# Sums over masked keys in an attention stage: two float32r passes over the high and low parts of the values, split by GpSimd batch by batch

## What is computed

```python
def _L0_xattn_ref(value, key, query, mask, Wv, bv, Wk, bk, Wq, bq, Wo, bo):
    v = (value @ Wv.T + bv).reshape(n, -1, H, D)
    k = (key @ Wk.T + bk).reshape(n, -1, H, D)
    q = (query @ Wq.T + bq).reshape(n, -1, H, D)
    qk = jnp.einsum('nqhd,nkhd->nhqk', q, k)
    qk = jnp.where(mask == 0, jnp.asarray(1e-20, qk.dtype), qk)
    attn = jax.nn.softmax(qk / jnp.asarray(np.sqrt(E), qk.dtype), axis=3)
    out = jnp.einsum('nhqk,nkhd->nqhd', attn, v).reshape(n, q_len, H * D)
    return out @ Wo.T + bo
...
x = x + _L0_xattn_ref(ctx_1024, ctx_1024, _layernorm(x, axis=-1), mask_Bx1xSxS2_ik1, ...)
```

## Time and profile before

| | |
|---|---|
| median of 3 runs | 4522.49 us (4519.5 to 4533.23) |
| span of the profiled execution, the only time of its own that the page gives | 4527.3 us |
| TensorE busy | 3886.3 us (86%) |
| VectorE busy | 3074.1 us (68%) |
| ScalarE busy | 2057.9 us (45%) |
| GpSimd busy | 795.1 us (18%) |
| granted TensorE clock, mean over the span | 0.907 |
| loop of the first attention | from 126.8 to about 772 us of the span |

### The profile page before, as it was taken

How to read it: one execution, slowest core, us unless ns; L and a number is a source line. 1 busy time by engine, 2 the same in 40 slices (tenths; PEclk the granted TensorE clock), 3 DMA queues, 4 the chain that set the end, 5 groups by cost and what they waited for, 6 DMA issues and landing times. The chain is left out here.

```text
span 4527.3 us, 83053 instructions
## 1 busy us (share of the span) xinstructions
PE 3886.3 (86%) x30431; PEld 2824.0 (62%) x30525; DVE 3074.1 (68%) x7110; ACT 2057.9 (45%) x3636; POOL 795.1 (18%) x510
## 2 busy tenths in 40 slices
PE   6799997799377999796399999779997987999899
PEld 5344443798365777575378888635555665555577
DVE  7666664456746666544566666678867887888587
ACT  3355554233103333342044444347775762777510
POOL 6433321401431000000023322410000013000000
PEclk9799999599668999897599999879998998999999
DMA  8233331201311000011054544722210015222000
GB/s 266 86 100 101 101 91 54 68 26 42 125 62 33 19 19 19 28 40 37 13 158 124 132 125 125 230 80 66 66 38 19 1 35 199 60 67 67 28 19 19
DMA packets 234478, 338.02 MB, mean 75 GB/s; under 512 B 39204, under 2 KB 132950, under 8 KB 234167
## 3 DMA queue, kind: packets, MB, share of 16 engines
q1 hardware_dynamic: 218280, 306.66, 21.4%
q0 software_dynamic: 15888, 27.23, 2.8%
HBM read 242.42 MB, written 107.01 MB: 77 GB/s over the span
## 5 line engine op out<-in xcount | busy, mean ns | idle before, releaser
L1918 ACT ACTIVATE a_pT<-a_psS 128x512 f32<-128x512 f32 x1536 | 836.0, 597 | 387.7 <-PE a_psS L1804 382.4
L1990 DVE TENSOR_REDUCE a_mx<-a_psA 128x1 f32<-128x512 f32 x1024 | 656.4, 685 | 82.9 <-PE a_psA L1782 82.8
L1819 PE MATMUL a_psZ<-a_pT,a_V 128*17 128x128 f32 x12288 | 488.8, 278 | 0.0
L1782 PE MATMUL a_psA<-a_ks,a_qs 48*128 48x512 f32 (+1 forms) x1536 | 405.5, 523 | 83.8 <-DVE a_mx L1990 36.9
L1986 DVE CUSTOM_DVE_ANT_0 a_scored<-a_psA,a_hide_q 128x512 bf16<-128x512 f32 x512 | 332.7, 688 | 184.4 <-PE a_psA L1782 183.3
L1819 PEld LDWEIGHTS a_psZ<-a_pT,a_V 128*17 128x17 f32 x12288 | 272.8, 97 | 272.7 <-issue 163.3
L1782 PEld LDWEIGHTS a_psA<-a_ks,a_qs 48*128 48x128 f32 (+1 forms) x1536 | 151.6, 192 | 330.2 <-DVE a_mx L1990 127.7
L1804 PE MATMUL a_psS<-a_qs,a_ks 50*128 50x512 f32 (+1 forms) x1536 | 318.3, 408 | 2.7 <-ACT a_pT L1918 0.8
L3262 DVE SCALAR_TENSOR_TENSOR ex_h<-ex_psU,ex_ub,ex_sg 128x512 f32<-128x512 f32 x129 | 96.9, 751 | 189.3 <-PE ex_psU L159 182.3
L2002 POOL TENSOR_TENSOR X<-X,a_osb 128x512 f32<-128x512 f32 x48 | 61.1, 1278 | 935.3 <-ACT a_osb L1905 917.3
L3208 ACT CAST ex_w_h<-X 128x1024 fp32r<-128x1024 f32 x102 | 106.0, 1040 | 149.5 <-DMA X<-in_L_ffn_gw 145.7
(11 more groups left out here) (606 smaller groups left out, 10227.2 us busy)
## 6 DMA issues: line engine op xcount, KB each, us to landing
a_qs<-a_q_parts SPq DMA_DIRECT2D x576, 64.0 KB, 2.3
a_ks<-a_k_parts SPq DMA_DIRECT2D x576, 64.0 KB, 2.3
a_k_parts<-a_p_kp SPq DMA_DIRECT2D x96, 256.0 KB, 2.6
a_q_parts<-a_p_qp SPq DMA_DIRECT2D x96, 256.0 KB, 3.2
X<-in_L_ffn_gw SPq DMA_DIRECT2D x36, 512.0 KB, 4.4
X<-in_L_ffn_up_w SPq DMA_DIRECT2D x36, 512.0 KB, 3.3
X<-in_L_ffn_down_w SPq DMA_DIRECT2D x36, 512.0 KB, 3.8
top_rows<-blank_rows SPq DMA_DIRECT2D x32, 514.0 KB, 4.8
```

The source lines that it names most:

```text
L1782: nc.tensor.matmul(psA[:, unit(a, par) % 3], qs[r, g % ring, p % 2, q * P:(q + 1) * P], ks[r, g % ring, p % 2], start=True, stop=True).the ...
L1819: last = nc.tensor.matmul(psZ[q * VP:q * VP + VW, g % 2, j * P:(j + 1) * P], V[:, b, kt, g % NG * GH + j, :], pT[:, p % 2, par, kt, q * P: ...
L1918: nc.scalar.activation(pT[:, p % 2, par, kt, :], psS[:, unit(t, par) % 3], ACT.Exp).then_inc(exp_done, 1)
L1990: nc.vector.tensor_reduce(mx[:, p // 2 % 2, par, p % 2, q:q + 1], psA[:, unit(a, par) % 3], AX_X, ALU.max).then_inc(a_used, 1)
```

## The change

The sums' fp32 products become float32r products. `is_hidden` becomes a float32r tile (its values are 0 and 1). V of the batch is split into a high part `V_h` (V rounded to float32r) and a low part `V_l` = V − `V_h`, both 128 x 1088, and each key tile is multiplied by both, into the same sum. GpSimd makes the split, once at the start of the loop, ahead of the bias adds, and then once for each next batch, ahead of `key_mask`. `V_h` and `V_l` exist once, so the split of batch u + 1 waits for the last sums of batch u, as `key_mask` did. TensorE waits for it at the first sums of a batch.

```diff
-            is_hidden = sb("is_hidden", [P, TB, S])
+            is_hidden = sb("is_hidden", [P, TB, S], F32R)
...
         def key_hide(pool, b):
-            nc.gpsimd.tensor_scalar(hide_k[:, b % 2], is_hidden[:], HIDDEN, None, ALU.mult).then_inc(hide_k_ready, 1)
+            nc.gpsimd.tensor_scalar(hide_k[:, b % 2], is_hidden[:].bitcast(F32), HIDDEN, None, ALU.mult).then_inc(hide_k_ready, 1)
...
+            V_h, V_l = sb("V_h", [P, TB, H * VW], F32R), sb("V_l", [P, TB, H * VW], F32R)
+            v_split = sem("v_split")
...
+                        if q == 0:
+                            pe.wait_ge(v_split, 2 * (u + 1))
                         for kt in range(TB):
-                            last = nc.tensor.matmul(ps[:, 0:H * VW], is_hidden[:, kt, q * P:(q + 1) * P], V[:, u, kt],
-                                                    start=(kt == 0), stop=(kt == TB - 1))
+                            for n_, part in enumerate((V_h, V_l)):
+                                last = nc.tensor.matmul(ps[:, 0:H * VW], is_hidden[:, kt, q * P:(q + 1) * P], part[:, kt],
+                                                        start=(kt + n_ == 0), stop=(kt + n_ == TB))
...
+                def split_values(b):
+                    whole = V[:, b].rearrange("p t h v -> p t (h v)")
+                    nc.gpsimd.tensor_copy(V_h[:], whole).then_inc(v_split, 1)
+                    pool.wait_ge(v_split, 2 * b + 1)
+                    nc.gpsimd.tensor_tensor(V_l[:], whole, V_h[:].bitcast(F32), ALU.subtract).then_inc(v_split, 1)
+
+                if hidden is not None:
+                    split_values(0)
                 for b in range(B):
...
                 for u in range(B):
                     if hidden is not None and u + 1 < B:
                         pool.wait_ge(x_free, number["sums", TB * u + TB - 1] + 1)
+                        split_values(u + 1)
                         key_mask(pool, u + 1)
```

## The result

The changed kernel takes 4546.9 us (median of 4 runs, 4542.1 to 4552.2), the kernel before 4524.8 in the same series. The ratio is 1.0037, with a 95% interval of 1.0024 to 1.0051: slower by 11 to 23 us. I had forecast 4527, no change that can be told, and a range up to 4543. As a time the median lies 4 us above that range; taken by the ratio, from the 4522.5 that I had started from, it is 4539 and lies within it. The direction of my sum was right. Its mechanism was right in kind (GpSimd's displaced instructions hold one of VectorE's, and TensorE waits for it), and wrong in which instruction is held, in six of seven batches.

What follows compares the result with a forecast made beforehand. TensorE was taken to bound the first attention's steady loop. Sums −25.5, opening −3.9 and seven meetings of L1940 with hide_k +34.3 gave +4.9 us: 4527 us, range 4495 to 4543.

Steps and rivals of the forecast that it cites:

- Removed, the sums: Steady loop of the first attention: 28 sums as eight float32r products each, 0.91 us less per sum, 25.5 us less.
- Removed in the opening: First four sums: 7.0 us less, minus 3.1 for waits among the later bias adds; 3.9 us less, between 0 and 7.
- The split itself costs nothing, its place does: GpSimd between batches: cast 1.3 and subtraction 2.5 us fit idle time, but push key_mask and key_hide by 3.9 us.
- L1940 thus meets `hide_k` near its start: VectorE behind a batch's last sums: L1940 waits 4.4 us, not 0.4, so TensorE's L1833 begins 3.7 us later.
- seven such meetings: Trace before the change: L1956, two inputs in SBUF, unheld at 0.44 us while GpSimd made is_hidden; taken as evidence against the rule.
- The price of a meeting: Each of seven batches: 3.7 us of TensorE's wait plus 1.2 us of lower clock, 34.3 us more in all.
- The sum: Whole kernel: −25.5 − 3.9 + 34.3 = +4.9 us, 4527 us on the median, no change a measurement can tell.
- my own case: Main forecast, L1940 held by hide_k in seven batches: 4527 us, ends −10 to +18, 4512 to 4540; chance 0.57.
- The one that I gave 0.03: Rival: L1956 and L1960 each held for whole GpSimd instructions, 4 us more in each batch, 4555 us; chance 0.03.
- The slow cast: Rival: cast at L1642's rate, subtraction holds L1956 1.7 us, L1940 still meets hide_k; +20, 4542 us; chance 0.15.
- the products that aren't faster: Rival: float32r products with 272 columns go at the fp32 pace, nothing gained; +34, 4557 us; chance 0.05.
- the meetings go away: Rival: L1940 falls between or ahead of GpSimd's mask instructions and runs in 0.17 us; −31, 4491 us; chance 0.20.

Runs made afterwards that it cites:

- the two with memsets: The kernel before, with four memsets or one of a spare tile on GpSimd ahead of key_mask of batches 1 to 7: 4560.9 us and 4541.9 us.

## Why the prediction was right or wrong

- **Removed, the sums.** I had 28 x 0.91 = 25.5 us. By the batch without these waits (the split behind `key_hide`) it is 74.71 − 71.39 = 3.3 us, 7 x 3.3 = 23. The pace of 0.1275 was near (the last seven of the eight starts lie 0.12 to 0.13 apart); what I left out is that the first product of a group doesn't start its successor as quickly: 329.18 to 329.41, 0.23 us, so eight take 1.11.
- **Removed in the opening.** I had 3.9. It is less: by the run with the split behind `key_hide` the loop gained 24.3 in all, so 1.3 beside the 23. The four sums themselves gained 6.1 us there (3.92 to 2.11 three times, 2.65 to 1.97), where I had 7.0. What I left out is the clock: from the start of the loop to 170 us it was at its lower level for 37.5 us before, and for 44.4 in the changed kernel, without a break. That this took the rest is likely, and not shown by itself. From the loop's start to the first instruction behind the adds, the old opening took 42.6 to 44.9 us in the five traces that share it (mean 43.7) and the new one 43.5 to 43.8 in six: nothing gained that these traces can show. The waits among the bias adds came as I had them, to L1947's end at 147.08 (I had 147.0), but L1942's is short and L1945's and L1947's are whole ones:

```profile
142.53 2.26 DVE L1945 TENSOR_SCALAR a_nparts<-a_mx 128x16 fp32r<-128x16 f32 x1
...
144.82 2.26 DVE L1947 SCALAR_TENSOR_TENSOR a_nparts<-a_mx,a_nparts 128x16 fp32r<-128x16 f32 x1
...
147.18 0.45 PE L1835 MATMUL a_psZ<-ident,a_nparts 128*128 128x128 f32 x1 [4.70 <-DVE a_nparts L1947]
```

- **The split itself costs nothing, its place does.** Right, and the run without a split shows it, but for one meeting in batch 0, in one trace of six. The cast took 1.09 us (I had 1.3, from two rows of other sizes), the subtraction 2.51 (2.50).
- **"L1940 thus meets `hide_k` near its start."** This is the step that failed. In six of seven batches L1961, three steps of the loop earlier, met L1637 first, was held for 3.39 to 3.47 us, and by its lateness L1945 came behind `hide_k` and wasn't held. I had put L1956 aside because a row showed it at 0.44 us in the midst of L1637. The row was right and my reading of it too wide: it came 3.75 us behind L1637's start, and the hold lasts for 3.5. It was free by a quarter of a microsecond. I wrote of seven such meetings. The trace has six (in batch 0 L1956 doesn't fall into L1637), all at nearly the same distance, 3.69 to 3.75 us, and I took them for as many proofs; they were one.
- **The price of a meeting.** By luck it was nearly the same: TensorE stood for 3.35 to 3.43 us (I had 3.7), and 3.99 in batch 0. What comes behind the wait cost more than my 1.2: batches of 76.35 and 77.29 us against 71.39 are 5.0 and 5.9 more, so beside the waits there are 1.6 to 2.6 us in each, which I put down to the lower clock (behind waits of 1.03 us, with no lower clock, a batch was 1.0 longer and no more). Seven meetings cost 41.8 us by the loops (39.4 by the medians of the two runs), where I had 34.3. Some 2 us of it are in the loop's end, whose last products ran at the lower clock for 10.2 us and not 3.4.
- **The sum.** −25.5 − 3.9 + 34.3 = +4.9 became −23 − 1.3 + 41.8 = +17.5 in the loops of the profiles (661.7 against 619.9, and 619.9 against 644.2), and +22 between the medians (17 by the ratio, 11 to 23 by its interval). All three terms were off to the same side. Together they come to the upper end that I had worked out for my own case, +18, though by another instruction's wait and a clock that cost more than my end of 1.8 in most batches.
- **The rivals.** The one that I gave 0.03, L1956 held as the rule has it, is the nearest to what came, at 4547 us and not at the 4555 that I worked out: L1961 is held, but only to 3.5 us and not to the end of L1637, and the one behind it, L1965, isn't held. I weighed the rule against a row that contradicts its length and not its kind. The Trainium skill, SBUF — State Buffer, section SBUF: two separate sides, states that a VectorE instruction with two inputs in SBUF and a GpSimd instruction that reads SBUF exclude each other for the whole instruction. By the runs this holds in its kind: L1961 with two inputs in SBUF was held by L1637, L1958 with one in PSUM wasn't, and L1957 began 0.2 us before the end of a memset, which reads nothing, and took its 0.44 us. In its length it doesn't hold for two inputs (3.5 of 5.4 us). The one-input `tensor_scalar` was held to the end (5.23 of 5.37). The slow cast and the products that aren't faster didn't come. Nor did the meetings go away in this kernel; moving one call does that.

## What to carry to other kernels

Work that is hidden by itself can still cost more than its whole gain by what it moves: look at what comes behind it in its queue, and at which instructions of VectorE and GpSimd will then start together. The 0.82 us that a sum gained were real, and four of them were outweighed by one meeting of 3.4 us with the lower clock behind it. Put added GpSimd work behind the instructions whose place is already free, not ahead of them, and look at the new place as well: behind `key_hide` the split met L1942 in one of the six traces that have it there. And when a row is to show that two instructions don't disturb each other, note how far into the first the second began: it says so for that distance only.

## What the runs showed of the hardware that I had not expected

A `tensor_scalar` of 128x2048 on GpSimd takes 5.37 us, but holds an instruction of VectorE's with two inputs in SBUF only for the first 3.5 of them: the same in the three traces in which such a one came early (the changed kernel and the two with memsets), for L1637 (int32 to float32 or float32r) and L1642 (float32 to bfloat16). One that came 3.69 us or more behind the start was held in none of the traces. Whether this is a fixed time or two thirds of the instruction isn't shown, since both take 5.37 us; a `tensor_tensor` of GpSimd's (2.51 us) held one to 0.15 us before its own end. A one-input `tensor_scalar` of VectorE's, 128x16, is held until the GpSimd instruction is done (5.23 of 5.37 us, 7.03 of 7.09). Waits of TensorE of 1.02 to 1.11 us in a dense loop left the granted clock at 1.00 (2.4 GHz) six times of six; waits of 2.54 to 2.60 us and of 3.35 to 3.43 us were followed by 0.50 (1.2 GHz) for 3.4 or 6.8 us, twelve times of twelve.
